# Attention kernel on Trainium2: the transposes of outputs and of negated maxima go through the maxima's PSUM banks

## The reference, cut to what matters

```python
q = rope(split_heads(x @ W_q))          # 16 heads, 4096 queries, 16 wide
k = rope(split_heads(...)); v = split_heads(...)
scores = einsum('bhqd,bhkd->bhqk', q, k) / sqrt(16)
scores = where(causal, scores, -inf)    # layer 0 only
attn = softmax(scores, axis=-1)
out = einsum('bhqk,bhkd->bhqd', attn, v)
```

## Time and profile before

| what | value |
|---|---|
| median of 3 runs | 5106.11 us (5089.62 to 5106.27) |
| the profiled execution's own time | 5106.96 us |
| its span, first to last instruction | 5105.2 us |
| PE busy | 4890.6 us, 96% |
| DVE busy | 4444.0 us, 87% |
| ACT busy | 3781.3 us, 74% |
| granted TensorE clock, mean of the span | 0.967 of full |
| maxima's reductions (L1529) | 3200, 3724.3 us |
| transposes of negated maxima (L1384) | 70 |
| copies of transposed maxima on ACT (L1485) | 70, 18.6 us |
| copies of transposed outputs on ACT (L1515) | 58 full ones, 34.6 us |

### The profile page before, as it was taken

One profiled execution on the slowest core, in us unless ns is written; L12 is line 12 of the kernel. 1 busy time (PEld: TensorE's weight loads), 2 busy tenths in 40 slices (PEclk: granted clock), 3 DMA queues, 4 the chain that ended last, 5 costly groups with the idle time before them and its releaser, 6 DMA issues. The chain is left out here.

```text
span 5105.2 us, 103667 instructions
## 1 busy us (share of the span) xinstructions
PE 4890.6 (96%) x42852; PEld 2041.1 (40%) x42852; DVE 4444.0 (87%) x5078; ACT 3781.3 (74%) x7207; POOL 375.3 (7%) x546
## 2 busy tenths in 40 slices
PE   8799999999999899779999999999999999999998
PEld 5333333333333466434443333333333333333443
DVE  7799988988876599479999999999999999998346
ACT  3377887887887433338888888888888888888853
POOL 4100000000000233300000000000000000000120
PEclk9699999999999899979999999999999999999999
DMA  6301010010000000430001010000100000000000
GB/s 192 92 11 38 8 41 8 14 41 8 14 8 2 15 14 9 160 88 6 6 11 41 8 34 12 5 8 8 35 11 7 5 8 5 8 4 2 9 1 33
DMA packets 140172, 131.52 MB, mean 26 GB/s; under 512 B 62389, under 2 KB 99573, under 8 KB 139701
## 3 DMA queue, kind: packets, MB, share of 16 engines
q1 hardware_dynamic: 130724, 119.03, 7.8%
q10 hardware_dynamic: 8976, 5.86, 0.7%
HBM read 76.75 MB, written 46.66 MB: 24 GB/s over the span
## 5 line engine op out<-in xcount | busy, mean ns | idle before, releaser
L1529 DVE TENSOR_REDUCE att_mx<-ps 128x2 f32<-128x1024 f32 (+2 forms) x3200 | 3724.3, 1192 | 267.1 <-PE ps L1367 169.8
L1506 ACT ACTIVATE att_probs<-ps 128x512 f32<-128x512 f32 (+3 forms) x6400 | 3378.4, 583 | 623.8 <-PE ps L1430 273.6
L1470 PE MATMUL ps<-att_probs,att_V 128*17 128x256 f32 (+1 forms) x22016 | 1722.1, 387 | 0.3 <-ACT att_outT L1522 0.2
L1430 PE MATMUL ps<-att_Q,K 50*128 50x512 f32 (+3 forms) x5632 | 1457.9, 490 | 23.1 <-ACT att_probs L1506 22.1
L1367 PE MATMUL ps<-K,att_Q 48*128 48x512 f32 (+3 forms) x6400 | 1363.5, 407 | 74.8 <-DVE att_mx L1529 41.5
L1430 PEld LDWEIGHTS ps<-att_Q,K 50*128 50x128 f32 x5632 | 566.8, 184 | 1191.3 <-ACT att_probs L1506 1100.7
L1470 PEld LDWEIGHTS ps<-att_probs,att_V 128*17 128x17 f32 x22016 | 373.6, 96 | 918.6 <-issue 510.6
L1367 PEld LDWEIGHTS ps<-K,att_Q 48*128 48x128 f32 x6400 | 645.3, 190 | 151.9 <-DVE att_mx L1529 107.0
L1461 PE MATMUL ps<-att_probs,att_V 128*17 128x256 f32 x3072 | 238.9, 387 | 0.1
L1425 PE MATMUL ps<-att_Q,K 50*128 50x256 f32 x1536 | 206.5, 330 | 1.3 <-ACT att_probs L1506 1.3
L1866 POOL MEMSET mix_power<- 128x1 f32 x1 | 0.1, 98 | 2642.6 <-POOLq L132 2642.6
(11 more groups left out here) (216 smaller groups left out, 2589.1 us busy)
## 6 DMA issues: line engine op xcount, KB each, us to landing
att_Q<-qhi_scratch SPq DMA_DIRECT2D x232, 64.0 KB, 2.3
K<-khi_scratch SPq DMA_DIRECT2D x212, 64.0 KB, 2.3
v_scratch<-proj_vpad SPq DMA_DIRECT2D x16, 544.0 KB, 4.1
att_Q<-qlo_scratch SPq DMA_DIRECT2D x116, 64.0 KB, 2.3
att_V<-v_scratch SPq DMA_DIRECT2D x53, 136.0 KB, 2.4
K<-klo_scratch SPq DMA_DIRECT2D x106, 64.0 KB, 2.3
att_Q<-att_negT SPq DMA_DIRECT2D x280, 4.0 KB
proj_x<-in_L_attn_x SPq DMA_DIRECT2D x8, 512.0 KB, 6.5
```

The lines of the kernel that those rows point to most:

```text
L1430: mm = pe.matmul(ring(at)[:, lo:QB], K[rows, par_of(u), j, kt * P:(kt + 1) * P], Q[rows, slot_of(u), j, lo:QB], start=True, stop=True)
L1470: mm = pe.matmul(ps[VW * h:VW * h + HV, 6, lo:(part + 1) * (QB // 2)], V[:, par_of(v), kt, HV * h:HV * (h + 1)], probs[:, (n_key[v] + kt) ...
L1506: act.activation(probs[:, (n_key[u] + kt) % PBUFS, h if half_wide(u) else column(h), lo:QB], ring(at)[:, lo:QB], ACT.Exp, scale=SCALE).the ...
L1529: dve.tensor_reduce(mx[:, u % 2, :, j, qt, c], ps[:, 2 + 2 * pair:4 + 2 * pair, 0:max_width(u, i) // 2], AX.X, ALU.max).then_inc(max_taken, 1)
```

## The change

The transposes leave the scores' ring. `RING` is gone, and only `score` takes a place in the ring. The steps `max`, `turn_max` and `turn_out` now form one queue in the order in which they stand in the lists (`number`), and each takes the next of the two pairs of banks, by its number's parity (`pair_of`). A transpose uses the first bank of its pair. So TensorE may write entry n of the queue, of whichever kind, when entry n-2 has been read by VectorE.

VectorE now reads the transposes where they are. It copies the negated maxima out of PSUM (`keep_turned`, a 32x128 `tensor_copy`) and takes reciprocal and product straight from the bank. ScalarE's two copies (L1485, L1515) are gone, and with them the tile `att_out`. `att_outT` and `att_rden` have two buffers. SyncE's DMAs of the negated maxima wait for `max_taken` instead of `emptied`.

TensorE's order of instructions is the same as before. The diff, cut to its core:

```diff
-    RING = ("score", "turn_max", "turn_out")
...
-            at_ring += step[0] in RING
+            at_ring += step[0] == "score"
...
+    queue = first_queue + [step for u in range(UNITS) for step in plan[u] if step[0] in ("max", "turn_max", "turn_out")]
+    number = {step: n for n, step in enumerate(queue)}
+    def pair_of(step):
+        return number[step] % 2
...
-                def place_max(turned_at, u):
-                    sp.wait_ge(emptied, turned_at + 4)
+                def place_max(u):
+                    sp.wait_ge(max_taken, number["turn_max", u] + 3)
...
-                def take_max(i, u, at, pair):
+                def take_max(u, i):
                     j, qt, c = maxima(u)[i]
-                    pe.wait_ge(max_taken, at + 1)
+                    pair = pair_of(("max", u, i))
+                    pe.wait_ge(max_taken, number["max", u, i] + 1)
...
-                def turn_max(count, at):
-                    pe.wait_ge(neg_steps, count * NEG_STEPS + NEG_STEPS)
-                    pe.transpose(ring(at)[:, 0:P], negp[:], ident[:]).then_inc(scored, 1)
+                def turn_max(u):
+                    step = ("turn_max", u)
+                    pe.wait_ge(max_taken, number[step] + 1)
+                    pe.wait_ge(neg_steps, u * NEG_STEPS + NEG_STEPS)
+                    pe.transpose(ps[:, 2 + 2 * pair_of(step), 0:P], negp[:], ident[:]).then_inc(max_scored, 1)
+
+                def turn_out(v):
+                    step = ("turn_out", v)
+                    pe.wait_ge(max_taken, number[step] + 1)
+                    pe.wait_ge(out_kept, v + 2)
+                    for t in range(tiles(v)):
+                        mm = pe.transpose(ps[:, 2 + 2 * pair_of(step), t * P:(t + 1) * P], outT[:, v % 2, t * P:(t + 1) * P], ident[:])
+                    mm.then_inc(max_scored, 1)
...
-                        elif what == "turn_max":
-                            w = step[1]
-                            if w >= 2:
-                                act.wait_ge(max_got[w % 2], 64 * (w // 2))
-                            keep_turned(w % 2, at)
-                        elif what == "turn_out":
-                            n = tiles(step[1])
-                            act.activation(out[:, 0:n].rearrange("p t h e -> p (t h e)"), ring(at)[:, 0:n * P], ACT.Copy
-                                           ).then_inc(emptied, 1)
...
+                def keep_turned(u):
+                    step = ("turn_max", u)
+                    dve.wait_ge(max_scored, number[step] + 1)
+                    if u >= 2:
+                        dve.wait_ge(max_got[u % 2], 64 * (u // 2))
+                    dve.tensor_copy(negT[:, u % 2, :], ps[0:PARTS * NEG, 2 + 2 * pair_of(step), 0:P]).then_inc(max_taken, 1)
...
                         elif step[0] == "turn_out":
                             v = step[1]
-                            dve.wait_ge(emptied, at + 4)
                             n = tiles(v)
-                            dve.reciprocal(rden[:, 0:n], out[:, 0:n, :, HD]).then_inc(out_recip, 1)
+                            out = ps[:, 2 + 2 * pair_of(step), 0:n * P].rearrange("p (t h e) -> p t h e", t=n, h=GH)
+                            dve.wait_ge(max_scored, number[step] + 1)
+                            dve.reciprocal(rden[:, v % 2, 0:n], out[:, :, :, HD]).then_inc(out_recip, 1)
...
-                                ALU.mult).then_inc(out_read, 1)
+                                ALU.mult).then_inc(max_taken, 1)
```

More of the change, by code:

```diff
@@ L1122, in attention @@
     upto = list(accumulate(len(maxima(u)) for u in range(UNITS)))
-    max_number = {item: n for n, item in enumerate(items)}
     n_before = upto[0] + AT_START
@@ L1218, in attention, with last_max @@
         n_key.append(n_key[-1] + keys(u))
-    turned_at = {step[1]: at for u in range(UNITS) for step, at in zip(plan[u], place[u]) if step[0] == "turn_max"}
-    turned_at[0] = -1
+    first_queue = []
+    for n, (w, i) in enumerate(items[0:n_before]):
+        first_queue.append(("max", w, i))
+        if n == len(maxima(0)) + AFTER_GATHER // 2 - 1:
+            first_queue.append(("turn_max", 0))
+    queue = first_queue + [step for u in range(UNITS) for step in plan[u] if step[0] in ("max", "turn_max", "turn_out")]
+    number = {step: n for n, step in enumerate(queue)}
+    assert len(number) == len(queue)
+    def pair_of(step):
+        return number[step] % 2
+    def last_max(u):
+        return "max", u, len(maxima(u)) - 1
     NEG = GH * QT
@@ L1239, in attention @@
         probs = sb("probs", [P, PBUFS, GH, QB])
-        outT = sb("outT", [P, QB])
-        out = sb("out", [P, QT, GH, VW])
+        outT = sb("outT", [P, 2, QB])
         mx = sb("mx", [P, 2, 2, PAIRS, QT, NQB])
@@ L1334, in _ @@
                     load_queries(w)
[L1335 removed]
+                place_max(0)
                 for u in range(UNITS):
@@ L1406, in _ @@
                     if n == len(maxima(0)) + AFTER_GATHER // 2 - 1:
-                        turn_max(0, -1)
+                        turn_max(0)
                 pe.wait_ge(neg_set, 3)
@@ L1414, in _ @@
                         what = step[0]
-                        if what in RING:
+                        if what == "score":
                             pe.wait_ge(emptied, at + 1)
@@ L1441, in _ @@
                             first_keys(w, i)
-                            take_max(i, w, max_number[w, i], max_number[w, i] % 2)
+                            take_max(w, i)
                         elif what == "turn_max":
-                            turn_max(step[1], at)
+                            turn_max(step[1])
                         elif what == "values":
@@ L1476, in _ @@
                         elif what == "turn_out":
[L1477 to L1480, removed]
+                            turn_out(step[1])
             @block.scalar
             def _(act):
-                def keep_turned(par, at):
-                    act.activation(negT[:, par, :], ring(at)[0:PARTS * NEG, 0:P], ACT.Copy).then_inc(emptied, 1)
                 for piece in range(FIRST if causal else NQB):
                     fetch_keys(act, 0, piece, k_first[piece], v_first[piece])
-                act.sem_inc(emptied, 2)
+                act.sem_inc(emptied, 3)
                 act.sem_inc(out_kept, 1)
-                act.wait_ge(scored, 1)
-                keep_turned(0, -1)
                 for u in range(UNITS):
@@ L1519, in _, with reduce_max @@
                             act.wait_ge(values_done, n_key[v + 1] + PBUFS)
+                            if v >= 2:
+                                act.wait_ge(max_scored, number["turn_out", v - 2] + 1)
                             n = tiles(v) * P
-                            act.activation(outT[:, 0:n], ps[:, 6, 0:n], ACT.Copy).then_inc(out_kept, 1)
+                            act.activation(outT[:, v % 2, 0:n], ps[:, 6, 0:n], ACT.Copy).then_inc(out_kept, 1)
             @block.vector
             def _(dve):
-                def reduce_max(i, u, at, pair):
+                def reduce_max(u, i):
                     j, qt, c = maxima(u)[i]
-                    dve.wait_ge(max_scored, at + 1)
+                    pair = pair_of(("max", u, i))
+                    dve.wait_ge(max_scored, number["max", u, i] + 1)
                     dve.tensor_reduce(mx[:, u % 2, :, j, qt, c],
@@ L1538, in gather @@
                     if u:
-                        dve.wait_ge(scored, turned_at[u - 1] + 2)
+                        dve.wait_ge(max_scored, number["turn_max", u - 1] + 1)
                     steps.link(dve.tensor_copy(negp[:, 0:NEG].bitcast(F32R), neg[:]))
@@ L1548, in _ @@
                 dve.sem_inc(max_taken, 2)
-                dve.sem_inc(out_read, 1)
                 for n, (w, i) in enumerate(items[0:n_before]):
-                    reduce_max(i, w, n, n % 2)
+                    reduce_max(w, i)
                     if n == len(maxima(0)) - 1:
                         gather(0)
+                    if n == len(maxima(0)) + AFTER_GATHER // 2 - 1:
+                        keep_turned(0)
                 for u in range(UNITS):
@@ L1569, in _ @@
                                 o_all[:, first_tile(v):first_tile(v) + n, cols].rearrange("p t (h d) -> p t h d", h=GH),
-                                out[:, 0:n, :, 0:HD], rden[:, 0:n].unsqueeze(3).to_broadcast([P, n, GH, HD]),
-                                ALU.mult).then_inc(out_read, 1)
+                                out[:, :, :, 0:HD], rden[:, v % 2, 0:n].unsqueeze(3).to_broadcast([P, n, GH, HD]),
+                                ALU.mult).then_inc(max_taken, 1)
 LN_STEPS = 4
```

16 lines of the change are left out of this document (8 added, 8 removed).

## The result

The changed kernel took 5150.87 us in the median (5139.54 to 5157.82, 4 executions), the kernel before beside it 5097.86 us (5082.64 to 5106.27, 4 executions). The ratio is 1.0105 with a 95% interval of 1.0071 to 1.0139: slower by about 1%, or 53 us. A second series of the same kernel (`e_again`) gave 5149.0 us against 5101.22, ratio 1.0096 (1.0078 to 1.0115). The profiled execution's span is 5137.7 us against 5105.2, so this one pair, at nearly the same mean granted clock (0.968 and 0.967), differs by 32.5 us.

A forecast was written before the change was run, and what follows sets the result against it. TensorE was taken to bound the kernel. Stalls 40.9 us plus longer matmuls 4.6 less 1.5 for ScalarE made +44 on 5106.96: 5151, 5150 on the median's scale, less 2 for absorbed layer 0 stalls: 5148 us, range 5118 to 5162.

The forecast's parts named there:

- TensorE sets the pace: Undisturbed rounds: TensorE starts items every 1.22 us; VectorE can manage 1.13, so only TensorE's delays cost their full length.
- Stall at the turn_max: Layer 1: next item's matmuls wait 0.67 us for a reduction, plus 0.10 longer matmuls; 34 of 38 places lose, sum 22.8.
- half-wide turn_outs: Half-wide units have two transposes, not four, so the next item waits, for example 0.13 us; 10 units, sum 2.0 us.
- the longer matmuls: On TensorE, a pair that has waited takes 0.50 against 0.40 us; 0.10 at some 46 places, 4.6 us.
- Turn_out of full units costs nothing, the added copy nothing, PSUM reads nothing: Turn_out margin 0.10 us, cost 0; VectorE's 0.27 us copy a unit falls in idle time; PSUM reads run beside TensorE's work.
- Layer 0's stalls, 16 us: Layer 0: 18 of 32 turn_max lose 13.2 us in sum, 4 lose 1.0, and 4 early turn_outs lose 1.9.
- what ScalarE's copies cost: Removing ScalarE's copies of 0.27 and 0.60 us a unit gains 1.5 us in all, 0.02 a unit, bounded by 0 and 4.
- the first rival: Layer 0's 22 stalls (14.2 us) and layer 1's half-wide ones vanish in other TensorE waits: 5124 us; chance 0.12.
- Rival 2 (VectorE binds): VectorE sets the pace, so turn_out decides: -0.27 us a unit, -19, 5088 us; chance 0.08 together with rival 4.
- 3 (the turn_outs stall): Some 45 full units' turn_outs lose 0.1 us and 0.1 for longer matmuls: +9, 5157, up to 5165 us; chance 0.10.
- 4 (TensorE catches up): After each stall TensorE catches up using ScalarE's freed time; no size given; chance 0.08 together with rival 2.

The follow-up runs named there:

- e_copy2: The changed kernel with VectorE copying the transposed maxima twice, the first into a scratch tile; ratio 1.0082 to the kernel before.
- e_out_only: The changed kernel with turn_max put back in the scores' ring with ScalarE's copy, only turn_out in the new queue; ratio 1.0013 to the kernel before.
- c_spread: The kernel before, with one reduction between each two of the gather's three VectorE instructions; ratio 1.0036 to the kernel before.

## Why the prediction was right, point by point

- *TensorE sets the pace.* Right. Adding VectorE work in its idle time changed nothing (e_copy2), and rounds of 1.22 us stood in every kernel. The Trainium skill's "Perfetto Trace Analysis" (section "Identifying the Most-Contended Engine") takes occupancy as a fair measure for Vector; here 98.7% occupancy hid 7% of room, and the measured intervals decide.
- *Stall at the turn_max: 0.67 and 0.10 a place.* Right: 2.26 instead of 1.60, and 1.33 instead of 1.23; 0.76 a unit. The full units are 23, not 22; the sum of 22.8 has them all. Layer 1's attention gave +26.6 us; the places summed to 22.8 for the turn_max and 2.0 for half-wide turn_outs, with about 3.5 for the longer matmuls, 28.
- *Turn_out of full units costs nothing, the added copy nothing, PSUM reads nothing.* Right (e_out_only +1, e_copy2). The Trainium skill's "VectorE: DVE Perf Modes" (section on the TRN2 errata) gives 120 fixed cycles for PSUM sources and 58 for SBUF; the trace has 254 ns for the reciprocal from PSUM and 253 from SBUF, so no such difference shows in the records here.
- *Layer 0's stalls, 16 us.* The stalls themselves came as read (0.67 to 0.69 more at 432.6, 588.2, 1034.2 and the like), but this is the term that was mis-sized: at equal clock layer 0 gave 9. Two things give time back. Where a turn_max stands in a gap, its place in the scores' ring had held up the next round's second score, as in c_spread. The prediction valued what ScalarE's copies cost, at 0.02 a unit, but had no term for the place in the ring. Before, around the matmuls of the earlier trace rows at 1147.87, and after (TensorE alone: transpose, scores, items):

```profile
1147.18 0.33 PE L1384 MATMUL ps<-ident,att_negp 128*128 128x128 f32 x1
1147.44 0.92 PE L1430 MATMUL ps<-att_Q,K 50*128 50x512 f32 x2
...
1149.42 0.41 PE L1367 MATMUL ps<-K,att_Q 48*128 48x512 f32 x2
```

```profile
1153.72 0.33 PE L1396 MATMUL ps<-ident,att_negp 128*128 128x128 f32 x1
1153.98 0.50 PE L1451 MATMUL ps<-att_Q,K 50*128 50x512 f32 x2
1154.32 0.40 PE L1377 MATMUL ps<-K,att_Q 48*128 48x512 f32 x2
...
1155.54 0.39 PE L1377 MATMUL ps<-K,att_Q 48*128 48x512 f32 x2
```

  From the transposes (1147.18 and 1153.72) to the second item are 2.24 and 1.82 us: 0.42 won, at five such places. Before, the exponentials and the second score there were:

```profile
1146.73 1.08 ACT L1506 ACTIVATE att_probs<-ps 128x512 f32<-128x512 f32 x2
1147.70 0.26 ACT L1485 ACTIVATE att_negT<-ps 32x128 fp32r<-32x128 f32 x1
```

```profile
1147.87 0.49 PE L1430 MATMUL ps<-att_Q,K 50*128 50x512 f32 x1
```

  The score starts 0.06 after the exponentials' end (1147.81) and before the copy's end (1147.96). And at three other turn_max of layer 0 (813, 962 and 1188) the next three distances between items gave back about half a microsecond of the stall, most likely since TensorE would have waited there anyway: the first rival, in part. Added up over the distances around each turn_max of layer 0 (from e_again's profile where a stretch at the lower clock disturbs the first), what was lost less what came back is about 9 us.
- *The time.* 5148 forecast, 5150.87 measured; that they lie 3 us apart is in part luck. The forecast was 42 us above the 5106.11 from which it started, while the change cost 53 us against the kernel before beside it, and 48 in e_again. Three errors cancel in part: the stalls, less what came back, are 36 us and not 42; 8 to 11 us go with a lower clock, which I had not thought of; and the starting point lay 4 us above the 5102.0 that 57 executions of before gave.
- *Rival 2 (VectorE binds), 3 (the turn_outs stall), 4 (TensorE catches up)* did not come.

## What to carry to other kernels

Two buffers in turn are a promise about order: whatever is put between two users of the pair makes the second depend on the one just before, and not on the one before that. With three buffers in turn it is the same, one place further back. Put a small extra user into such a queue only where the reader is on time, and look for what makes it late just ahead of that place. When you move such a user by a planner, count what else the planner moved. Read the pace from the distances between starts, undisturbed and in a backlog; an engine that is 98% busy may still be the one that follows.

## What was not expected of the hardware

In layer 0 TensorE is granted the lower clock (1.2 GHz, 0.5 in the records) in short stretches, many of which lie elsewhere in each execution, and one such stretch can cost as much as a third of the whole change. In the profiled execution of e_out_only one lasted 41 us from 1077 us on; the same units in the kernel before had almost none:

```profile
1069.00:1153.00 84.00, 82.14 (x679) 30.04 (x678) 60.09 (x62) 53.34 (x106) 2.54 (x4) 0.76 0.17 43
```

```profile
1059.00:1128.00 69.00, 67.47 (x661) 25.75 (x660) 60.63 (x58) 55.94 (x110) 2.54 (x4) 0.98 0.25 69
```

The first row is e_out_only, the second before; the granted clock is 0.76 and 0.98, and that unit took 15.8 us longer (88.1 against 72.3). In layer 1's full units the clock did not fall in any of the twelve profiles, though with the change TensorE waited 0.7 us once a unit. Kernels that differ in layer 0 only by some waits of TensorE or VectorE had mean clocks from 0.9647 (c_spread) to 0.9683 (before). What decides it was not found out.
